# Two graph layers on one core: loading x group by group, and when the adjacency gathers may begin

## What is computed

```python
def graph_mean(x, adj, weight, bias):              # first layer
    a = adj.astype(x.dtype)
    x1 = a @ x / sum(a, axis=1)
    return concatenate([x1, x], axis=1) @ weight + bias

def attention(x, adj, W, a):                       # second layer
    h = x @ W.T
    e = (h @ a[:128])[:, None] + (h @ a[128:])[None, :]
    e = where(adj == 0, -inf, e)
    return softmax(e, axis=1) @ h

x   = layernorm(x + graph_mean(x, adj, weight, bias))
out = layernorm(x + attention(x, adj, W, a))
```

## Time and profile before

| | |
|---|---|
| time, median of 3 runs | 1070.46 us |
| time of the profiled execution | 1069.98 us |
| its span, first to last instruction | 1068.2 us |
| TensorE busy | 1005.0 us (94%) |
| VectorE busy | 677.5 us (63%) |
| ScalarE busy | 611.6 us (57%) |
| DMA, mean over the span | 286 GB/s, 305.35 MB |
| TensorE's granted clock, mean | 0.979 |

### The profile page before, as it was taken

One profiled execution on the slowest core, in us unless ns is written; L12 is line 12 of the kernel. 1 busy time (PEld: TensorE's weight loads), 2 busy tenths in 40 slices (PEclk: granted clock), 3 DMA queues, 4 the chain that ended last, 5 costly groups with the idle time before them and its releaser, 6 DMA issues.

```text
span 1068.2 us, 22037 instructions
## 1 busy us (share of the span) xinstructions
PE 1005.0 (94%) x8783; PEld 876.4 (82%) x8783; DVE 677.5 (63%) x1599; ACT 611.6 (57%) x630; POOL 284.5 (27%) x277
## 2 busy tenths in 40 slices
PE   4789989889889999999999999999999999999996
PEld 4778867778778888888888888888888888888885
DVE  1566767877767677767676576555544656656654
ACT  1597879888888888888768676757421100000000
POOL 4044534434534344334333322322000000000000
PEclk8889999999999999999999999999999999999999
DMA  9489999999999999999999999999130012222011
GB/s 295 179 340 415 422 421 422 420 423 420 422 421 421 422 417 412 421 420 422 400 391 360 352 342 344 348 324 324 63 127 10 26 61 85 85 85 81 19 39 32
DMA packets 51177, 305.35 MB, mean 286 GB/s; under 512 B 6624, under 2 KB 7904, under 8 KB 17536
## 3 DMA queue, kind: packets, MB, share of 16 engines
q0 software_dynamic: 37472, 270.42, 64.0%
q1 hardware_dynamic: 13136, 33.19, 9.0%
q10 hardware_dynamic: 464, 0.30, 0.1%
HBM read 286.29 MB, written 17.59 MB: 284 GB/s over the span
## 4 chain that ended last, share of the span: by engine, by line
PE 63%; DMA 26%; ACT 6%; issue 2%; DVE 1%; SPq 0%; POOL 0%; ACTq 0%; DVEq 0%
PE ps_agg L344 34%; DMA adj_in<-in_adj_dram,chunk 24%; PE ps_part L344 23%; ACT edges L503 5%; PE ps_y L344 4%; DMA bias<-in_L_gnn_bias_dram 2%; PE ps_h L627 1%; PE ps_h L689 1%; DVE partial L823 0%; PE ps_x1T L682 0%; SPq L380 0%; ACT parts L495 0%; POOL adj_in L1254 0%; DVE edgesT L854 0%; DVE packed L867 0%
## 5 line engine op out<-in xcount | busy, mean ns | idle before, releaser
L344 PE MATMUL ps_agg<-parts,edgesT 128*128 128x257 f16 (+1 forms) x5312 | 617.4, 276 | 31.5 <-DVE edgesT L854 31.5
L344 PEld LDWEIGHTS ps_agg<-parts,edgesT 128*128 128x128 fp8e4 x5312 | 521.5, 99 | 114.8 <-DVE edgesT L854 36.0
L503 ACT ACTIVATE edges<-adj_in 128x2048 fp8e4<-128x2048 int32 x256 | 480.5, 1904 | 61.6 <-DMA adj_in<-in_adj_dram,chunk 59.5
L1254 POOL DMA_INDIRECT adj_in<-in_adj_dram,chunk x256 | 278.4, 1087 | 457.6 <-ACT edges L503 446.1
L854 DVE STREAM_TRANSPOSE edgesT<-edges 128x512 uint32<-128x512 uint32 x256 | 168.0, 691 | 75.0 <-ACT edges L503 74.3
L344 PE MATMUL ps_part<-parts,edgesT 128*128 128x258 f16 x1664 | 194.6, 274 | 0.0
L344 PEld LDWEIGHTS ps_part<-parts,edgesT 128*128 128x128 fp8e4 x1664 | 162.5, 98 | 22.9
L573 ACT ACTIVATE std<-mean_var,eps 128x1 f32<-128x1 f32 x64 | 18.9, 295 | 204.2 <-DVE mean_var L1075 204.2
L867 DVE SCALAR_TENSOR_TENSOR packed<-edgesT,packed 128x2048 uint32<-128x2048 uint32 x48 | 109.8, 2287 | 0.1
L344 PE MATMUL ps_part<-parts,packed 128*128 128x258 f16 x836 | 96.4, 273 | 0.0
L344 PEld LDWEIGHTS ps_part<-parts,packed 128*128 128x128 fp8e4 x836 | 81.6, 98 | 11.9
(11 more groups left out here) (118 smaller groups left out, 638.1 us busy)
## 6 DMA issues: line engine op xcount, KB each, us to landing
adj_in<-in_adj_dram,chunk POOLq DMA_INDIRECT x256
out_dram<-edges SPq DMA_DIRECT2D x60, 64.0 KB, 2.8
partial_sums<-partial SPq DMA_DIRECT2D x13, 258.0 KB
adj_in<-partial_sums SPq DMA_DIRECT2D x13, 258.0 KB, 5.9
packed_adj<-packed SPq DMA_DIRECT2D x3, 1024.0 KB
adj_in<-packed_adj SPq DMA_DIRECT2D x2, 1024.0 KB, 6.5
x_all<-in_x_dram SPq DMA_DIRECT2D x6, 256.0 KB, 16.4
x_all<-in_x_dram POOLq DMA_DIRECT2D x6, 256.0 KB
```

The costliest lines, as they stand in the source:

```text
L344: done = eng.matmul(bank[:, 0:cols], rows[:, n // BYTES, n % BYTES, :], moving[:, n, :], start=(n == first), stop=(n == last))
L503: act.activation(edges[:, r // 2, r % 2, :], adj_in[:, m % SLOTS, :], ACT.Copy, scale=EDGE[t % GROUP], saturate=False).then_inc(s_conv, 1)
L1254: pool.indirect_dma_start(adj_in[:, m % SLOTS, :], None, adj_chunks, bass.IndirectOffsetOnAxis(chunk[:, 0:1], 0), element_offset=first_row ...
```

## The change

The x transfers become 16, one for each group and all on SP's queue, each over all 128 partitions and with a semaphore of its own; `transpose_x(j)` waits for its own group. ScalarE's two and GpSimd's eight x transfers go. The transfer of the bias moves from SP's queue, where it stood behind x, to ScalarE's, behind `w0`. `keep_v(0)` and `keep_v(1)` move behind all groups in VectorE's program, and each `transpose(0, r)` of the first tile moves one turn back, the last behind the loop. GpSimd waits, ahead of its first gather, until group 11 of x (the twelfth) has landed. Each output group is stored in one transfer of 128 partitions in place of four; so are the two pieces of the last group, and ScalarE stores nothing.

The diff, with the unchanged context lines cut:

```diff
-    x_quarters = x.rearrange("(a s b w c) f -> s a w b (c f)", a=NQ, s=QUARTERS, b=NB // QUARTERS, w=QUAD, c=BYTES)
-    out_groups = out.rearrange("(a g w c) f -> g a w c f", a=NQ, w=QUAD, c=BYTES)
+    x_groups = x.rearrange("(a g w c) f -> g a w (c f)", a=NQ, w=QUAD, c=BYTES)
+    out_groups = out.rearrange("(a g w c) f -> g a w (c f)", a=NQ, w=QUAD, c=BYTES)
...
-    ALL_STORED = [16 * NQ * sum(1 for j in range(GROUPS - 1) if j % 4 == s) for s in range(4)]
+    ALL_STORED = [16 * sum(1 for j in range(GROUPS - 1) if j % 4 == s) for s in range(4)]
...
 sync:
-            for a in (0, 1):
-                sp.dma_start(x_all[QUAD * a:QUAD * (a + 1), 0:BYTES, :].rearrange("p c f -> p (c f)"),
-                             x_quarters[0, a][:, 0, :]).then_inc(s_xfirst, 16)
-            for s in range(QUARTERS):
-                for a in (0, 1):
...
-                        .then_inc(s_x[s], 16)
-            sp.dma_start(bias[:, :], b0.rearrange("(o f) -> o f", o=1).to_broadcast([P, F])).then_inc(s_bias, 16)
+            for j in range(GROUPS):
+                sp.dma_start(x_all[:, GROUP * j:GROUP * (j + 1), :].rearrange("p c f -> p (c f)"), x_groups[j])\
+                    .then_inc(s_x[j], 16)
...
-                for a in range(NQ):
-                    sp.dma_start(out_groups[loads[j], a], y_out[QUAD * a:QUAD * (a + 1), j % 4, :, :])\
-                        .then_inc(s_outst[j % 4], 16)
+                sp.dma_start(out_groups[loads[j]], y_out[:, j % 4, :, :].rearrange("p c f -> p (c f)"))\
+                    .then_inc(s_outst[j % 4], 16)
...
-            for a in (0, 1):
-                sp.dma_start(out_groups[loads[j], a, :, GROUP - 1, :],
-                             y_out[QUAD * a:QUAD * (a + 1), j % 4, GROUP - 1, :]).then_inc(s_outl, 16)
+            sp.dma_start(out_groups[loads[j], :, :, (GROUP - 1) * F:GROUP * F], y_out[:, j % 4, GROUP - 1, :])\
+                .then_inc(s_outl, 16)
...
 scalar:
-            for a in (2, 3):
-                act.dma_start(x_all[QUAD * a:QUAD * (a + 1), 0:BYTES, :].rearrange("p c f -> p (c f)"),
-                              x_quarters[0, a][:, 0, :]).then_inc(s_xfirst, 16)
             act.dma_start(w0_sb[:, :, :], w0.rearrange("(c p) f -> p c f", p=P)).then_inc(s_const, 16)
+            act.dma_start(bias[:, :], b0.rearrange("(o f) -> o f", o=1).to_broadcast([P, F])).then_inc(s_bias, 16)
...
-            act.wait_ge(s_out, TILES)
-            for a in (2, 3):
-                act.dma_start(out_groups[loads[GROUPS - 1], a, :, GROUP - 1, :],
-                              y_out[QUAD * a:QUAD * (a + 1), (GROUPS - 1) % 4, GROUP - 1, :]).then_inc(s_outl, 16)
...
 tensor:
-                if j == 0:
-                    pe.wait_ge(s_xfirst, 16 * NQ)
-                else:
-                    pe.wait_ge(s_x[j // QUARTERS], 16 * 2)
-                    pe.wait_ge(s_xp[j // QUARTERS], 16 * 2)
+                pe.wait_ge(s_x[j], 16)
...
 vector:
                 if j > 0:
                     split_u_lo(j - 1)
-                if 0 < j <= AHEAD:
-                    keep_v(j - 1)
-                if j in FIRST_AFTER:
-                    transpose(0, FIRST_AFTER.index(j))
+                if j - 1 in FIRST_AFTER:
+                    transpose(0, FIRST_AFTER.index(j - 1))
+            transpose(0, NQ - 1)
+            for j in range(AHEAD):
+                keep_v(j)
...
 gpsimd:
-            for s in range(QUARTERS):
-                for a in (2, 3):
-                    first = 1 if s == 0 else 0
-                    pool.dma_start(x_all[QUAD * a:QUAD * (a + 1), QBLK * s + BYTES * first:QBLK * (s + 1), :]
-                                   .rearrange("p (b c) f -> p b (c f)", c=BYTES), x_quarters[s, a][:, first:, :])\
-                        .then_inc(s_xp[s], 16)
             for a in range(NQ):
                 pool.iota(chunk[QUAD * a:QUAD * (a + 1), :], pattern=[[0, 1]], base=a,
                           channel_multiplier=NQ * BYTES).then_inc(s_chunk, 1)
                 pool.wait_ge(s_chunk, a + 1)
+            pool.wait_ge(s_x[GROUPS * 3 // 4 - 1], 16)
```

More of the change, by code:

```diff
@@ L199, in bass_two_graph_layers @@
         g_banks = [ps_agg[1], ps_small]
-        s_x = [sem(f"x_upper_landed{s}") for s in range(QUARTERS)]
-        s_xp = [sem(f"x_lower_landed{s}") for s in range(QUARTERS)]
-        s_xfirst = sem("x_first_words_landed")
+        s_x = [sem(f"x_landed{j}") for j in range(GROUPS)]
         s_const = sem("w0_landed")
@@ L367, in weighted_at @@
             return exponents_at(g) + 1
-        ALL_STORED = [16 * NQ * sum(1 for j in range(GROUPS - 1) if j % 4 == s) for s in range(4)]
+        ALL_STORED = [16 * sum(1 for j in range(GROUPS - 1) if j % 4 == s) for s in range(4)]
         @block.sync
         def _(sp):
-            for a in (0, 1):
-                sp.dma_start(x_all[QUAD * a:QUAD * (a + 1), 0:BYTES, :].rearrange("p c f -> p (c f)"),
-                             x_quarters[0, a][:, 0, :]).then_inc(s_xfirst, 16)
-            for s in range(QUARTERS):
-                for a in (0, 1):
-                    first = 1 if s == 0 else 0
-                    sp.dma_start(x_all[QUAD * a:QUAD * (a + 1), QBLK * s + BYTES * first:QBLK * (s + 1), :]
-                                 .rearrange("p (b c) f -> p b (c f)", c=BYTES), x_quarters[s, a][:, first:, :])\
-                        .then_inc(s_x[s], 16)
-            sp.dma_start(bias[:, :], b0.rearrange("(o f) -> o f", o=1).to_broadcast([P, F])).then_inc(s_bias, 16)
+            for j in range(GROUPS):
+                sp.dma_start(x_all[:, GROUP * j:GROUP * (j + 1), :].rearrange("p c f -> p (c f)"), x_groups[j])\
+                    .then_inc(s_x[j], 16)
             sp.dma_start(w1_sb[:, :], w1).then_inc(s_const1, 16)
@@ L437, in _ @@
             sp.wait_ge(s_out, TILES - 1)
-            for a in range(NQ):
-                sp.dma_start(out_groups[loads[j], a, :, 0:GROUP - 1, :],
-                             y_out[QUAD * a:QUAD * (a + 1), j % 4, 0:GROUP - 1, :]).then_inc(s_outl, 16)
+            sp.dma_start(out_groups[loads[j], :, :, 0:(GROUP - 1) * F],
+                         y_out[:, j % 4, 0:GROUP - 1, :].rearrange("p c f -> p (c f)")).then_inc(s_outl, 16)
             sp.wait_ge(s_out, TILES)
-            for a in (0, 1):
-                sp.dma_start(out_groups[loads[j], a, :, GROUP - 1, :],
-                             y_out[QUAD * a:QUAD * (a + 1), j % 4, GROUP - 1, :]).then_inc(s_outl, 16)
+            sp.dma_start(out_groups[loads[j], :, :, (GROUP - 1) * F:GROUP * F], y_out[:, j % 4, GROUP - 1, :])\
+                .then_inc(s_outl, 16)
             for s in range(4):
                 sp.wait_ge(s_outst[s], ALL_STORED[s])
-            sp.wait_ge(s_outl, 16 * 2 * NQ)
+            sp.wait_ge(s_outl, 16 * 2)
             sp.wait_ge(s_flag, 1)
@@ L1086, in rows_out @@
                 if c == 0:
-                    wait(dve, s_outst[j % 4], 16 * NQ * (j // 4))
+                    wait(dve, s_outst[j % 4], 16 * (j // 4))
                 dve.tensor_scalar(y_out[:, j % 4, c, :], z[:, u % 2, :], mean_var[:, u % 2, 0:1],
```

## The result

The changed kernel takes 1086.57 us (median of 5 runs, 1086.05 to 1086.84), the kernel before 1070.21 us in the runs beside it. The ratio is 1.0147, 95% interval 1.0134 to 1.0161: the changed kernel is slower by 16.4 us, well clear of noise. The span of the profiled execution grew from 1068.2 to 1084.8 us.

The account below looks back on a forecast made before the run. Bound: full DMA gather stream, then TensorE, without slack. Tenth gather 14.0 us later plus 0.5 for output gives +14.5: 1069.98 becomes 1084.5, 1085.0 as median; range 1077 to 1105 us.

Parts of the forecast that it names:

- The bound, and the tenth gather as the measure: Whole kernel: gather stream, then TensorE, neither with slack; the end moves with the tenth gather's issue, 58.94 us before.
- Four engines: x load: slowest count of 4 puts each transfer on four DMA engines, 32 packets each, not sixteen with 8.
- Price of a packet: x load: 87 ns per 2 KB packet, bounds 78 and 128; 2.8 us per group, group 11 landed at 36.2 us.
- Beside the gathers: After group 11: x and gathers alternate packets, 2.5 us per gather; convert(0, 0) ends at 43.1 us, group 15 lands at 67.2.
- From group 15 to the tenth gather: End of first tile: ScalarE, held by convert(0, 2), needs 5.7 us more; tenth gather at 72.9 us, 14.0 later.
- Bias and VectorE's order hide behind the late x: First part: the 13.79 us bias stall goes, but moved transposes and keep_v gain nothing while x is late.
- Rival A: x load: sixteen engines carry each transfer, all of x in 11.2 us, time 1047.8 us; chance 0.16.
- effective start of the stream: Gather stream: tenth gather's data less nine gathers of 2.49 us; 37.8 us before, rival A 13.4, or up to 19.
- Output: Stores: merged transfers cost nothing until the end, there between -0.7 and +1.5 us, taken as +0.5.
- SP's issues: SP's queue: 16 x issues of about 0.43 us within 8 us, at most 6 to 14 us, ahead of the data.

Follow-up runs that it names:

- the fast load: Changed kernel with x in 32 transfers by quarter and pair of groups, sixteen engines: 1055.22 us with GpSimd's wait for twelve groups, 1066.54 us without.
- the new order: Kernel before with only VectorE's order changed (bias sums behind all groups, first tile's transposes one turn later): 1052.39 us; with GpSimd's twelve-group wait added, 1052.97 us.
- the halves: Changed kernel with each x transfer cut in two halves of 64 partitions: 1129.12 us, ratio 1.0543.
- the pairs: Changed kernel with x in 32 transfers on SP's queue, each a quarter of the partitions and two groups, wait for twelve groups kept: 1055.22 us, ratio 0.9851.

## Why the prediction was right

The forecast was 1085.0, the time is 1086.57; +14.5 us were foreseen and 16.4 measured. The mechanism is as forecast, four engines for x and a tenth gather that waits for it. That the size came out so close is in part luck, as several terms erred in opposite ways. By its steps:

- *The bound, and the tenth gather as the measure.* Right; the table shows it over a range of 77 us.
- *Four engines.* Right: 0.27 of 16 engines is 4.3, and 0.13 is two for a count of two.
- *Price of a packet.* 87 ns were put, 2.57 us per group over 32 packets is 80 ns: near the lower bound. Group 11 landed in time for a gather at 36.92 us, 36.3 were forecast. Twelve groups of cheaper packets save 2.8 us, and the start uses them up: the first group was forecast for 5.4 us and transposed only at 7.75.
- *Beside the gathers* it was dearer than put. The first conversion, waiting for the first gather, began at 46.85 us, 41.2 were forecast; group 14 was there at 54, group 15 at 67.5. I had 64 and 67.2. The end of x agrees by errors of opposite sign: packets 7 ns cheaper alone, against a late start and 348 GB/s in place of 421 while the gathers and x are mixed (44 to 67 us). The forecast's even alternation of packets is not what the middle groups show.
- *From group 15 to the tenth gather:* 5.7 us forecast, 7.2 measured, by another way than forecast. ScalarE was not held by `convert(0, 2)`, which had begun at 57.48 us; TensorE's products were the path. TensorE, busy for 4.87 of the 23 us from 44 to 67 us, was granted 0.51 there, its lower level of 1.2 GHz, and 0.50 on until 71 us. The two dense products behind group 15's transposes took 1.91 and 1.87 us where one takes 1.16 at the upper level. These 1.5 us are the size of what the term lacked.
- *Bias and VectorE's order hide behind the late x.* Right: no wait on the bias is left, and with x on time the two, with the output, are worth 16 us. Rival A gave 1047.8 for 16 engines, 1055.2 were measured. Its place was right and its size off: it put the effective start of the stream at 13 to 19 us, and the tenth gather's data at 43.65 + 1.3 less nine gathers of 2.49 put it at 22.5. A packet cost 132 ns and not 87, and the first conversion began at 30.12 us where the rival had 21.
- *Output.* +0.5 us put. From the last issue to the end the run with the output alone has 0.4 us more and the changed kernel (1078.99 to 1084.8 us) 0.5; the times can't tell it from nothing.
- *SP's issues* were said to be done within 14 us. They took 34 us, 2.44 us each: SP was held at an issue for about as long as the four engines needed for a group. `w1` and `a2` so went out at 35 to 40 us and TensorE waited 0.73 us for them. That was not foreseen; it cost next to nothing here, but in a kernel with other work on SP it would.

## What to carry to other kernels

Before merging transfers, look at the slowest count on both sides of the pattern: here, by the DMA shares, one transfer of 4 x 32 pieces ran on four DMA engines where transfers with a slowest count of 32 ran on sixteen, and that turned a gain of 16 us into a loss of 16. A load and a stream that share slots and engines are ordered by what frees the slots: holding the stream back until its consumer's input is there was worth 11 us with the fast load, and nothing with the load of before and the new order. And a wait placed ahead of later groups' work on an in-order engine can be paid for by moving its consumer, not its transfer: the new order alone, with the bias as late as ever, gave a time that no other run beat.

## What was not expected of the hardware

- SP's issue of a transfer took 2.44 us (median) with x on four engines, and 2.44 us again for the halves on two, whose 128 KB take 2.57 us there. With x on sixteen (the pairs) all 32 issues took 0.40 to 0.43 us.
- The same pattern from GpSimd's queue used all engines (share 1.05), at 206 GB/s and with 2454 packets under 512 B in 14 us.
- The x packets on four engines cost 80 ns each, and still 80 ns on two (64 packets in 5.1 us by 51 GB/s), but 132 ns on sixteen in the pairs run (249 GB/s from 10 to 20 us, mostly before the first gather's data), close to the 128 ns of the crowded start before. So sixteen engines carried x 2.4 times as fast as four, and not four times. Why a packet is dearer with sixteen is open.
